# Cross-attention planner: rank by reader backlog, new places for the side work, values wait for their context

## The chip, the cores and the metric

The kernel runs on one core of a Trainium2 chip. The time is device time in microseconds (us), the median over several executions; less is better. The engines of the core are TensorE (PE; its weight loads are PEld), VectorE (DVE), ScalarE (ACT), GpSimd (POOL), and SyncE (SP), which here issues all DMAs. [...]

## What is computed

Two decoder layers over 16 batch elements. `x` is (16, 256, 128), the context `ctx_1024` is (16, 1601, 128), all float32. There are 16 heads of 8.

```python
# layer 0
x = layernorm(x + attn(x, x, x, causal))
x = layernorm(x + attn(x, ctx, ctx))                 # 256 queries, 1601 keys
x = layernorm(x + moe(x))                            # 8 experts of 512, top 2, exact gelu
# layer 1
h = x + mha(rmsnorm(x), rmsnorm(x), rmsnorm(x), self_mask)
h = h + mha(rmsnorm(h), ctx, ctx, cross_mask)
out = h + moe_ffn(rmsnorm(h))                        # 8 silu experts, top 2, and one shared expert
```

Every softmax is an exact one with its row maximum taken off; the experts are computed densely and weighted (`comb`), with zero weight for those not picked.

## The kernel before, in words

The work is cut into rounds, t = -1 to 32. Round t does the cross-attention of one batch element (layer 0 for t = 0 to 15, layer 1 for t = 16 to 31) and beside it side work for its neighbours: the experts of the element of round t-1, and for the element of round t+1 the self-attention, the keys, the values, the moves of the keys and, in layer 1, the masks; loads of `x` and of the context for round t+2.

The cross-attention is the backbone. For each of four head groups g (four heads) and each of seven pairs of key tiles i there is a beat of four score tiles `SC` [g.i] (line 939; in layer 1 a mask is put in first by line 929), whose readers are exponentials on ACT (`probs_c`, line 1226), and one or two steps `WV` that add the sums of the pair before (line 957). The row maxima that these scores need come one round earlier, from chunks `MC` (line 828): scores once more, in the other orientation, read by DVE as maxima (line 1069 in layer 0, line 1075 in layer 1, where the mask is added). There are 96 chunks of 512 keys and 16 tails of 68 keys in a round. A matmul of `SC` or `MC` uses 32 of the 128 rows of the array, so four heads run at the same time.

Other step names: `XT` transposes `x` (846) for ACT to copy; `QP` makes queries and keys of the self-attention and the queries of the cross-attention from it (852), which DVE adds a bias to and POOL splits in two; `KC` and `VC` make keys and values from the context (986, 990); `KD` moves the keys of one head group by twelve DMAs (1335); `MS`, `SS`, `WS` are maxima, scores and sums of the self-attention (873 to 913); `OT`, `OPT`, `OPM` transpose and project an attention's result; `EF` and `ES` are the two halves of an expert (1016, 1028), whose weights are loaded by `EL` (1347) into two slots each; `CL` loads the context (1325).

Seven PSUM banks are shared by all steps but the sums. A step waits until the reader of its bank's last user (DVE for some kinds, ACT for others) is done. All engines run their instructions in the program's order.

The order is set while the program is built, by a planner. `weave` holds one queue of steps for each kind of side work and one for the backbone, spreads each queue over the round by the table `WHEN` (begin and end as shares of the round, times `LENGTH`), and takes step after step: among the heads of the queues that are within `AHEAD` us of the earliest due one, the one with the least `idle + NEAR * place`, where `idle` comes from `Model`, a cost model of TensorE, its readers and the banks. To each beat it adds up to `MOST` chunks `MC` while banks are free in the model within `SOON` us; and `behind`, with `SLACK` chunks of tolerance, adds a beat of chunks alone after a score beat when the maxima are late.

The lines of the planner that matter:

```python
            trial = Model(model)
            idle = sum(trial.add(x) for x in piece)
            if best is None or idle + NEAR * place < best[0]:
                best = idle + NEAR * place, which
```

Of the kernel before, what the change touches and what calls it, by code (L numbers as in the profile page):

```python
# [65 lines left out]
def spans(n, step):  # L66
    return [(a, min(step, n - a)) for a in range(0, n, step)]
# [83 lines left out]
BY_READER = {"OPM": ("x_in", "mid", "stored"), "EBM": ("xe",), "ES": ("xe", "comb"), "MC": ("mask",)}  # L151


LENGTH = (145.1, 143.0)


class Model:
# [128 lines left out]

NEAR, AHEAD, SOON, MOST, SLACK = 0.0485, 53.3, 0.42, 4, 4


def weave(plan, length, *lists):
# [4 lines left out]
    for begin, end, steps in lists:  # L297
        timed = spaced(steps)
        total, done, queue = sum(cost for _, cost in timed), 0.0, []
        for x, cost in timed:  # L300
            place = length * (begin + (end - begin) * (done + cost_of(x) / 2) / total)
# [28 lines left out]
    while any(queues):  # L330
        follow()
        soonest = min(queue[-1][0] for queue in queues if queue)
        best = None
        for which, queue in enumerate(queues):
            if not queue or queue[-1][0] > soonest + AHEAD:
                continue
            place, piece = queue[-1]
            own = {id(x) for x in piece}
            if any(id(y) in pending - own for x in piece for y in x.of.values()):
                continue  # L340
            trial = Model(model)
            idle = sum(trial.add(x) for x in piece)
            if best is None or idle + NEAR * place < best[0]:
                best = idle + NEAR * place, which
        if best is None:
            steps = [plan.follow.pop(0)] if plan.follow else beat_of(plan.pull(model, pending, MOST, True))
            put(steps)
            continue
        _, piece = queues[best[1]].pop()
        put(piece)  # L350
        scores = [x for x in piece if x.kind == "SC"]
        if scores and plan.behind(scores[-1]):
            follow()
            steps = plan.pull(model, pending, MOST)
            if steps:
                put(beat_of(steps))
# [3 lines left out]
def beat_of(steps):  # L360

    for n, x in enumerate(steps):
        x.beat, x.led = steps, n > 0
    return steps
# [309 lines left out]
def numbered(order):  # L674
# [4 lines left out]
    for x in order:  # L679
# [22 lines left out]
    return order  # L702


WHEN = [{"experts": (0.3, 1.0), "keys": (0.049, 0.375), "values": (0.21, 0.706), "self": (0.01, 0.692), "load": (0.398, 0.739), "context": (0.914, 0.924)},
        {"experts": (0.114, 0.97), "keys": (0.124, 0.276), "values": (0, 0.439), "self": (0.029, 0.786), "load": (0.507, 0.886), "context": (0.775, 0.876), "cross masks": (0.283, 0.787), "self masks": (0.764, 0.88)}]


def round_of(plan, t):

    side = []
    if t >= 1:
        begin, end = WHEN[(t - 1) // B]["experts"]
        side += [(begin, end, plan.experts((t - 1) // B, (t - 1) % 2)),
                 (end, end + 0.01, plan.store((t - 1) % 2, (t - 1) % B))]
    if t + 1 < LAST:
        l, p, b = (t + 1) // B, (t + 1) % 2, (t + 1) % B
        when = WHEN[l]
        if t < 0:
# [18 lines left out]
    if t < 0:  # L738
        return weave(plan, LENGTH[0], *side) + plan.first_maxima()
    if t == LAST:  # L740
        sums = plan.last_sums()
        for x in sums:
            plan.model.add(x)
        return sums + weave(plan, LENGTH[1], *side)
    return weave(plan, LENGTH[t // B], (0, 1, attended), *side)


# [20 lines left out]
def nth(x):  # L768

    return x.n + 1  # L770
# [62 lines left out]
def tensor_program(pe, T, M, order):  # L833
    for x in order:
# [148 lines left out]
        elif x.kind == "KC":  # L983
            if "ctx" in x.of:
                pe.wait_ge(M["ctx_loaded"], 16 * nth(x.of["ctx"]))
            pe.matmul(tile[:, 0:x.kn], T["w_key"][:, x.l, :], T["ctxT"][:, x.k0:x.k0 + x.kn], start=True,
                      stop=True).then_inc(M["d_made"], 1)
        elif x.kind == "VC":
            for n, (k0, kn) in enumerate(spans(SK, P)[x.i:x.i + 3]):
                last = pe.matmul(tile[0:kn, n * VCOLS:(n + 1) * VCOLS], T["ctxT"][:, k0:k0 + kn], T["w_val"][:, x.l, 1, :],  # L990
                                 start=True, stop=True)
# [18 lines left out]
        elif x.kind == "EF":  # L1010
            load = x.of["load"]
# [7 lines left out]
        elif x.kind == "ES":  # L1019
            load, hid = x.of["load"], T["hidden"][x.i % 2]  # L1020
# [589 lines left out]
```

## Time and profile before

| | us |
|---|---|
| median of 3 executions | 4880.08 |
| lowest, highest | 4859.92, 4895.96 |
| the profiled execution, whole | 4873.83 |
| its span in the trace | 4872.4 |

| engine | busy us | share of the span |
|---|---|---|
| PE | 4629.5 | 95% |
| PEld | 2838.4 | 58% |
| DVE | 3616.2 | 74% |
| ACT | 2697.6 | 55% |
| POOL | 698.4 | 14% |

A busy PE is not PE at its peak, since matmuls overlap and their ends are modelled. [...] Where a wait is put down to an engine that had long been done, a DMA is what ended it.

### The profile page before, as it was taken

The page shows a single profiled execution, that of the slowest core. Times are in us where ns is not written, and L with a number is a line of the kernel's source. Part 1 is how long each engine was busy: PE and PEld are TensorE (multiplying, and loading weights), DVE is VectorE, ACT ScalarE, POOL GpSimd, SP SyncE. Part 2 cuts the span into 40 slices and gives each one's busy share as a digit, 9 for nine tenths or more (in the row PEclk, how much of TensorE's full clock was granted, in tenths as well). Part 3 has the DMA queues.
Part 4 walks back from the last instruction along what each step waited for, and adds up shares of the span by engine and source line. Part 5 has one row for each costly group of instructions (what it writes and reads, how often), then busy time and mean ns, then how long its engine had stood idle before and what let it go on. Part 6 is the DMA issues. An engine that isn't in the chain of part 4 may idle for free.

```text
span 4872.4 us, 105117 instructions
## 1 busy us (share of the span) xinstructions
PE 4629.5 (95%) x41312; PEld 2838.4 (58%) x41312; DVE 3616.2 (74%) x9823; ACT 2697.6 (55%) x5505; POOL 698.4 (14%) x853
## 2 busy tenths in 40 slices
PE   6999999999999999999999999999999999999999
PEld 3465556665556666555555556555565556655566
DVE  5766776667776767777667887778777887778875
ACT  1566556666666666665564544545455544555454
POOL 2111111211111221111111011011110111010100
PEclk8899999999999999999999999999999999999999
DMA  2122222222222222223333333323333223332322
GB/s 66 38 52 53 44 52 62 63 51 51 52 51 61 60 65 51 51 46 81 77 77 77 81 79 81 80 75 80 79 89 79 74 71 91 89 77 70 76 61 72
DMA packets 168007, 327.20 MB, mean 67 GB/s; under 512 B 25656, under 2 KB 76624, under 8 KB 167520
## 3 DMA queue, kind: packets, MB, share of 16 engines
q1 hardware_dynamic: 167520, 320.49, 26.9%
q8 instruction: 332, 5.44, 0.5%
q14 instruction: 155, 1.27, 0.1%
HBM read 237.40 MB, written 4.19 MB: 50 GB/s over the span
## 4 chain that ended last, share of the span: by engine, by line
PE 76%; DVE 18%; ACT 3%; issue 1%; POOL 0%; DMA 0%; DVEq 0%
PE sums L957 15%; PE b L1028 11%; PE b L1016 10%; PE b L828 9%; PE b L929 8%; PE b L939 7%; DVE chunk_max L1069 6%; PE b L852 4%; DVE b L1075 4%; DVE nm_s L1058 4%; PE b L913 2%; ACT probs_c L1226 2%; PE b L880 2%; PE b L904 1%; PE b L873 1%; PE b L885 1%
## 5 line engine op out<-in xcount | busy, mean ns | idle before, releaser
L1226 ACT ACTIVATE probs_c<-b 128x512 f32<-128x512 f32 (+1 forms) x3584 | 1737.5, 570 | 1368.1 <-PE b L939 1363.3
L1075 DVE CUSTOM_DVE_ANT_0 b<-b,mcross_q 128x512 f32<-128x512 f32 (+1 forms) x2048 | 1120.3, 606 | 234.8 <-PE b L828 230.9
L1069 DVE TENSOR_REDUCE chunk_max<-b 128x1 f32<-128x512 f32 x1536 | 969.1, 683 | 136.0 <-PE b L828 134.7
L957 PE MATMUL sums<-probs_c,vc 128*32 128x256 f32 x13312 | 932.7, 395 | 0.3 <-ACT probs_c L1226 0.3
L828 PE MATMUL b<-kc,qc 32*128 32x512 f32 (+1 forms) x4096 | 805.9, 411 | 15.3 <-DVE tmp_s L1087 2.0
L1028 PE MATMUL b<-w_back,hidden 128*128 128x128 f32 x4352 | 567.0, 283 | 25.5 <-DVE chunk_max L1069 20.2
L1028 PEld LDWEIGHTS b<-w_back,hidden 128*128 128x128 f32 x4352 | 536.5, 196 | 84.2 <-ACT probs_c L1226 31.4
L939 PE MATMUL b<-qc,kc 32*128 32x256 f32 (+1 forms) x6656 | 544.4, 339 | 29.2 <-DVE chunk_max L1069 11.4
L957 PEld LDWEIGHTS sums<-probs_c,vc 128*32 128x32 f32 x13312 | 347.2, 111 | 342.3 <-issue 160.5
L828 PEld LDWEIGHTS b<-kc,qc 32*128 32x128 f32 x4096 | 419.9, 187 | 213.1 <-ACT probs_c L1226 61.6
L1208 DVE SCALAR_TENSOR_TENSOR xe<-b,comb,xe 128x128 f32<-128x128 f32 x544 | 186.1, 349 | 478.0 <-PE b L1028 477.8
L1016 PE MATMUL b<-xT_e,w_in 128*128 128x256 f32 x2176 | 529.6, 388 | 7.0 <-ACT probs_s L1221 6.7
L939 PEld LDWEIGHTS b<-qc,kc 32*128 32x128 f32 (+1 forms) x6656 | 321.6, 183 | 339.0 <-issue 188.0
L929 PE MATMUL b<-mcross_k,ident_b 128*128 128x512 bf16 (+1 forms) x1792 | 469.2, 369 | 30.4 <-DVE k_lo L1126 8.0
L1016 PEld LDWEIGHTS b<-xT_e,w_in 128*128 128x128 f32 x2176 | 398.0, 191 | 95.6 <-ACT probs_c L1226 22.8
L1221 ACT ACTIVATE probs_s<-b 128x512 f32<-128x512 f32 x512 | 278.4, 597 | 257.8 <-PE b L891 257.2
L1058 DVE TENSOR_REDUCE nm_s<-b 128x2 f32<-128x512 f32 x512 | 329.0, 685 | 85.7 <-PE b L885 84.2
L929 PEld LDWEIGHTS b<-mcross_k,ident_b 128*128 128x128 bf16 (+1 forms) x1792 | 172.4, 100 | 231.0 <-DVE chunk_max L1075 60.2
L1075 DVE DVE_READ_ACCUMULATOR2_ANT chunk_max<- 128x1 f32 x2048 | 290.5, 142 | 0.0
L1249 ACT ACTIVATE hidden<-b 128x512 f32<-128x512 f32 x288 | 171.9, 597 | 165.4 <-PE b L1016 164.8
L1301 POOL TENSOR_TENSOR rstd_s<-mean_var_s,halves 128x2 f32<-128x2 f32 x32 | 31.6, 988 | 1590.7 <-DVE mean_var_s L1116 1590.7
L1245 ACT ACTIVATE hidden<-b,b_hid 128x256 f32<-128x256 f32 x512 | 206.4, 477 | 89.4 <-PE b L1016 87.3
(159 smaller groups left out, 4564.9 us busy)
## 6 DMA issues: line engine op xcount, KB each, us to landing
w_in<-in_experts SPq DMA_DIRECT2D x272, 256.0 KB, 3.3
w_back<-in_experts SPq DMA_DIRECT2D x272, 256.0 KB, 3.0
kc<-k_hi SPq DMA_DIRECT2D x1024, 50.0 KB
ctxT<-in_ctxT SPq DMA_DIRECT2D x32, 800.5 KB, 6.2
kc<-k_lo SPq DMA_DIRECT2D x512, 50.0 KB
mask_words<-in_mcross SPq DMA_DIRECT2D x32, 800.5 KB
mask_words<-in_mcrossT SPq DMA_DIRECT2D x32, 768.0 KB
out_x<-xe SPq DMA_DIRECT2D x32, 128.0 KB, 1.8
```

Of the source, the lines that this page charges most:

```text
L828: last = pe.matmul(tile[:, n * y.kn:(n + 1) * y.kn], T["qc"][y.p][rows, y.g, qt * P:(qt + 1) * P], T["kc"][rows, y.g, y.k0:y.k0 + y.kn], s ...
L929: pe.matmul(tile_of(T, y)[0:y.kn, 0:n * S], T["ident_b"][0:y.kn, 0:y.kn], mask, start=True, stop=False)
L939: last = pe.matmul(tile_of(T, y)[0:y.kn, half * S:(half + 1) * S], T["kc"][rows, y.g, kt * P:kt * P + y.kn], T["qc"][y.p][rows, y.g, :], s ...
L957: last = pe.matmul(acc[HP * j:HP * j + HP, :], T["vc"][x.p][0:x.kn, v0:v0 + HP], probs_of(T, x)[0:x.kn, j, half:half + S], start=x.j == 0, ...
L1016: last = pe.matmul(tile[:, half * S:(half + 1) * S], T["w_in"][load.slot][:, f * P:(f + 1) * P], T["xT_e"][:], start=True, stop=True)
L1028: last = pe.matmul(tile[:, 0:D], hid[:, f, x.c * P:(x.c + 1) * P], T["w_back"][load.slot][:, f * D:(f + 1) * D], start=f == 0, stop=f == N ...
L1058: dve.tensor_reduce(maxima[:, x.j, :, MROW], tile.rearrange("p (q k) -> p q k", q=QT), AX, ALU.max, negate=True).then_inc(M["d_read"], 1)
L1069: done = dve.tensor_reduce(best[:, x.i:x.i + 1], tile, AX, ALU.max)
L1075: done = dve.tensor_tensor_reduce(part, part, mask, 1.0, -3e38, ALU.add, ALU.max, best[:, qt:qt + 1])
L1221: act.activation(T["probs_s"][:, x.j, :], tile, ACT.Exp, scale=SCALE).then_inc(M["a_read"], 1)
L1226: act.activation(probs_of(T, x)[0:x.kn, x.j, 0:n], tile[0:x.kn, 0:n], ACT.Exp, scale=SCALE).then_inc(M["a_read"], 1)
L1245: done = act.activation(T["hidden"][x.i % 2][:, f, :], tile[:, half * S:(half + 1) * S], ACT.Gelu, bias=T["b_hid"][:, x.i, f:f + 1])
```

## The change

The planner's rank gains a term: after a trial it looks how far the clocks of DVE and ACT in the model are ahead of TensorE's by more than 1 us, and adds `HEAVY` times that. `DRY` would do the same for readers that are behind, and is 0. The constants and both tables are new (for layer 1 the context load moves from shares 0.775 to 0.876 of the round to 0.49 to 0.668), and `VC` now waits until its context has landed, where it is told which load that is; the number and shape of the matmuls, reads and DMAs are the same, and only their order differs.

```diff
-LENGTH = (145.1, 143.0)
+LENGTH = (140.4, 145.8)
...
-NEAR, AHEAD, SOON, MOST, SLACK = 0.0485, 53.3, 0.42, 4, 4
+NEAR, AHEAD, SOON, MOST, SLACK = 0.0436, 167.5, 0.32, 3, 2
+HEAVY, DRY = 0.091, 0
...
-            if best is None or idle + NEAR * place < best[0]:
-                best = idle + NEAR * place, which
+            rank = idle + NEAR * place
+            for busy in (trial.dve, trial.act):
+                rank += HEAVY * max(0, busy - trial.pe - 1.0) + DRY * max(0, trial.pe - busy)
+            if best is None or rank < best[0]:
+                best = rank, which
...
-WHEN = [{"experts": (0.3, 1.0), "keys": (0.049, 0.375), "values": (0.21, 0.706), "self": (0.01, 0.692), "load": (0.398, 0.739), "context": (0.914, 0.924)},
+WHEN = [{"experts": (0.207, 1.0), "keys": (0.177, 0.426), "values": (0.198, 0.975), "self": (0.08, 0.58), "load": (0.358, 1.0), "context": (0.95, 1.0)},
...
         elif x.kind == "VC":
+            if "ctx" in x.of:
+                pe.wait_ge(M["ctx_loaded"], 16 * nth(x.of["ctx"]))
```

The changed kernel's line numbers are 4 higher at the chunks, the scores and the sums (832, 943, 961), and 6 higher at values and experts (996, 1022, 1034). In the rows below `b` is a PSUM bank, `kc` and `qc` are the keys and queries of the cross-attention, and the number behind x counts matmuls.

**Place 1: TensorE in a steady round of layer 0, from the expert 6 to the second half of expert 7.** Before:

```order
L1028 MATMUL b<-w_back,hidden 128x128 x8
L939 MATMUL b<-qc,kc 128x256 x8
L828 MATMUL b<-kc,qc 128x512 x3
L957 MATMUL sums<-probs_c,vc 32x256 x4
L1028 MATMUL b<-w_back,hidden 128x128 x8
L939 MATMUL b<-qc,kc 128x256 x8
```

After:

```order
L1034 MATMUL b<-w_back,hidden 128x128 x8
L943 MATMUL b<-qc,kc 128x256 x8
L832 MATMUL b<-kc,qc 128x512 x3
L961 MATMUL sums<-probs_c,vc 32x256 x4
L996 MATMUL b<-w_val,ctxT 65x144
L1034 MATMUL b<-w_back,hidden 128x128 x4
L943 MATMUL b<-qc,kc 128x256 x8
L832 MATMUL b<-kc,qc 128x512 x3
L961 MATMUL sums<-probs_c,vc 32x256 x8
L1034 MATMUL b<-w_back,hidden 128x128 x4
```

Between the first half of expert 7 (`w_back`, x4 is one `ES` step) and the sums before it now stands the last, small piece of the values (`w_val`, 65x144), and the two `ES` steps of expert 7, which stood together, are a score beat apart. A few rows ahead, a beat of three chunks stands where the transposes of the maxima (`nm_c`) stood. The loads on SP stand in the same order in both programs: the twelve moves of head group 2, the `w_back` of expert 7, the context.

**Place 2: TensorE from the last maxima of a layer-0 round into the next round.** Before:

```order
L939 MATMUL b<-qc,kc 65x256 x4
L828 MATMUL b<-kc,qc 128x512 x2
L957 MATMUL sums<-probs_c,vc 32x256 x8
L904 MATMUL b<-ident,nm_c 128x128 x2
L828 MATMUL b<-kc,qc 128x512 x4
L846 MATMUL b<-ident,x_in 128x128 x2
L852 MATMUL b<-xT_s,w_pad 128x256 x2
L939 MATMUL b<-qc,kc 128x256 x8
L828 MATMUL b<-kc,qc 128x512
L957 MATMUL sums<-probs_c,vc 32x256 x4
L852 MATMUL b<-xT_s,w_pad 128x256 x6
L939 MATMUL b<-qc,kc 128x256 x8
```

After:

```order
L961 MATMUL sums<-probs_c,vc 32x256 x8
L908 MATMUL b<-ident,nm_c 128x128 x2
L832 MATMUL b<-kc,qc 128x512 x3
L850 MATMUL b<-ident,x_in 128x128 x2
L943 MATMUL b<-qc,kc 128x256 x8
L832 MATMUL b<-kc,qc 128x512
L961 MATMUL sums<-probs_c,vc 32x256 x4
L856 MATMUL b<-xT_s,w_pad 128x256 x2
L943 MATMUL b<-qc,kc 128x256 x8
L832 MATMUL b<-kc,qc 128x512 x2
L961 MATMUL sums<-probs_c,vc 32x256 x8
L856 MATMUL b<-xT_s,w_pad 128x256 x4
```

Before, the first projection (`w_pad`) stood right behind the transpose of `x_in`, and three more a beat later. Now a score beat and a sum stand between the transpose and the first projection, and the four come one, two and one, with score beats between.

**Place 3: TensorE in a steady round of layer 1, behind score beat [0.4].** Before:

```order
L828 MATMUL b<-kc,qc 128x512 x4
L975 MATMUL b<-ident,tmp_e 128x128 x2
L986 MATMUL b<-ctxT,w_key 128x401
L990 MATMUL b<-w_val,ctxT 128x144 x3
L980 MATMUL b<-w_out,oT_e 128x128 x2
L873 MATMUL b<-mself_q,ident_b 128x512 x2
L885 MATMUL b<-ks,qs 128x256 x4
L828 MATMUL b<-kc,qc 128x68 x4
L986 MATMUL b<-ctxT,w_key 128x398
L873 MATMUL b<-mself_q,ident_b 128x512 x2
L885 MATMUL b<-ks,qs 128x256 x4
L828 MATMUL b<-kc,qc 128x68 x4
```

After:

```order
L832 MATMUL b<-kc,qc 128x512 x2
L832 MATMUL b<-kc,qc 128x68 x2
L996 MATMUL b<-w_val,ctxT 128x144 x3
L984 MATMUL b<-w_out,oT_e 128x128 x2
L877 MATMUL b<-mself_q,ident_b 128x512 x2
L889 MATMUL b<-ks,qs 128x256 x4
L832 MATMUL b<-kc,qc 128x68 x6
L877 MATMUL b<-mself_q,ident_b 128x512 x2
L889 MATMUL b<-ks,qs 128x256 x4
L832 MATMUL b<-kc,qc 128x512
```

Before, two beats of self-attention maxima, two pieces of keys and two of values stood with eight tails and four chunks in a stretch without a score beat. Now one piece of values stands there, and the keys follow two score beats later, among the self-attention's scores. Over a round, beats that hold maxima chunks alone are 7 before and 11 after, in either layer.

## Rows read from the trace of the kernel before

**Rows 1.** The page: span, PE's total, PE's clock in 40 slices, the ending chain by engine.

```profile
span 4872.4 us, 105117 instructions
PE 4629.5 (95%) x41312; PEld 2838.4 (58%) x41312; DVE 3616.2 (74%) x9823; ACT 2697.6 (55%) x5505; POOL 698.4 (14%) x853
...
PEclk8899999999999999999999999999999999999999
...
PE 76%; DVE 18%; ACT 3%; issue 1%; POOL 0%; DMA 0%; DVEq 0%
```

**Rows 2.** The chain in order of time, a mark once a round: start, length, what.

```profile
384.05 3.58 DVE chunk_max L1069 x6
...
530.68 3.59 DVE chunk_max L1069 x6
...
1117.63 3.58 DVE chunk_max L1069 x6
...
1258.17 3.59 DVE chunk_max L1069 x6
```

**Rows 3.** Stretches, one round each: PE, PEld, DVE, ACT, POOL busy, clock, DMA share, GB/s.

```profile
660.70:807.20 146.50, 139.22 (x1231) 87.11 (x1227) 102.10 (x224) 90.45 (x184) 24.47 (x29) 0.94 0.24 54
...
1245.40:1384.90 139.50, 133.55 (x1230) 84.09 (x1226) 101.87 (x225) 90.46 (x184) 24.46 (x29) 0.99 0.25 57
...
3631.40:3785.20 153.80, 149.49 (x1361) 90.52 (x1357) 123.32 (x389) 77.95 (x160) 18.82 (x24) 1.00 0.31 80
```

**Rows 4.** Stretches, 3.4 us each, around the end of a layer-0 round.

```profile
800.35:803.76 3.41, 3.31 (x36) 1.93 (x32) 2.98 (x9) 3.07 (x8) 0.00 (x0) 0.91 0.00 0
803.76:807.18 3.42, 3.42 (x24) 1.18 (x22) 1.79 (x5) 0.19 (x1) 0.00 (x0) 0.50 0.41 45
...
814.00:817.42 3.42, 3.42 (x10) 2.50 (x8) 1.38 (x2) 0.00 (x0) 1.84 (x2) 0.59 0.81 292
817.42:820.83 3.41, 3.41 (x42) 2.04 (x41) 2.69 (x5) 2.57 (x6) 3.24 (x5) 1.00 0.01 2
```

**Rows 5.** Timeline of SP, 770 to 783 us: the moves of a head group, then loads.

```profile
773.66 0.65 SPq L1335 DMA_DIRECT2D kc<-k_hi  x1
...
782.16 0.44 SPq L1347 DMA_DIRECT2D w_back<-in_experts  x1
782.70 0.56 SPq L1325 DMA_DIRECT2D ctxT<-in_ctxT  x1
```

**Rows 6.** Timeline of PE, 781 to 800 us.

```profile
783.62 0.64 PE L957 MATMUL sums<-probs_c,vc 65*32 65x256 f32 x8
785.78 3.50 PE L1028 MATMUL b<-w_back,hidden 128*128 128x128 f32 x16 [1.52 <-DVE chunk_max L1069]
```

**Rows 7.** Issues 781 to 789 us: size, time to landing.

```profile
w_back<-in_experts SPq DMA_DIRECT2D x1, 256.0 KB, 3.5
```

**Rows 8.** Issues 3720 to 3722 us: a load behind a group's moves, no load after it.

```profile
w_in<-in_experts SPq DMA_DIRECT2D x1, 256.0 KB, 4.1
```

**Rows 9.** Issues 769.5 to 771 us: a load with no moves ahead of it.

```profile
w_back<-in_experts SPq DMA_DIRECT2D x1, 256.0 KB, 2.6
```

**Rows 10.** Timeline of PE, 806.5 to 818 us: the first projections of a round.

```profile
808.44 2.05 PE L852 MATMUL b<-xT_s,w_pad 128*128 128x256 f32 x4 [0.56 <-ACT xT_s L1219]
```

**Rows 11.** Timeline of PE: a beat of chunks alone, layer 0, and what follows.

```profile
1374.96 0.50 PE L828 MATMUL b<-kc,qc 32*128 32x512 f32 x4
1375.31 0.62 PE L939 MATMUL b<-qc,kc 32*128 32x256 f32 x3
```

**Rows 12.** The same in layer 1.

```profile
3770.29 0.51 PE L828 MATMUL b<-kc,qc 32*128 32x512 f32 x4
3770.73 1.56 PE L1016 MATMUL b<-xT_e,w_in 128*128 128x256 f32 x6
```

**Rows 13.** Stretches: the part of a round with the self-attention, layer 1 and layer 0.

```profile
3652.40:3688.90 36.50, 33.42 (x301) 17.06 (x299) 32.26 (x109) 16.81 (x37) 2.15 (x4) 1.00 0.18 41
...
1256.80:1315.10 58.30, 54.21 (x521) 28.73 (x520) 50.30 (x113) 31.65 (x68) 3.82 (x6) 1.00 0.09 13
```

**Rows 14.** Issues 3755 to 3762 us: the context load of layer 1.

```profile
ctxT<-in_ctxT SPq DMA_DIRECT2D x1, 800.5 KB, 6.9
```

More of the change, by code:

```diff
@@ L702, in numbered @@
     return order
-WHEN = [{"experts": (0.3, 1.0), "keys": (0.049, 0.375), "values": (0.21, 0.706), "self": (0.01, 0.692), "load": (0.398, 0.739), "context": (0.914, 0.924)},
-        {"experts": (0.114, 0.97), "keys": (0.124, 0.276), "values": (0, 0.439), "self": (0.029, 0.786), "load": (0.507, 0.886), "context": (0.775, 0.876), "cross masks": (0.283, 0.787), "self masks": (0.764, 0.88)}]
+WHEN = [{"experts": (0.207, 1.0), "keys": (0.177, 0.426), "values": (0.198, 0.975), "self": (0.08, 0.58), "load": (0.358, 1.0), "context": (0.95, 1.0)},
+        {"experts": (0.079, 1.0), "keys": (0.293, 0.368), "values": (0.119, 0.401), "self": (0.029, 0.629), "load": (0.5, 0.656), "context": (0.49, 0.668), "cross masks": (0.393, 0.779), "self masks": (0.786, 0.796)}]
 def round_of(plan, t):
```

## Prediction

> **What bounds the kernel now.** I read the page first. PE is busy in 95% of the span, and the chain that ended last runs over PE for 76% and over DVE for 18% [rows 1]. So PE is the bound, and DVE takes turns with it. The change adds and removes no matmul of the real work, so it can only win in three places: PE's idle time, time in which PE runs at half clock, and the small costs of turning from one kind of matmul to another.
>
> The marks of the chain give the length of a round in layer 0: 146.6 us from 384.05 to 530.68, the same mean over the next four (586.95 / 4 = 146.7), then 140.5 [rows 2]. The stretches by round say why. A round of 146.5 us had a granted clock of 0.94 and one of 139.5 us had 0.99, with the same busy time on DVE, ACT and POOL [rows 3]. A clock of 0.94 means 12% of 146.5, 17.6 us, at half speed, which loses 8.8; 0.99 means 2.8 us, which loses 1.4; 7.4 us between them, against 7.0 seen. So at full clock a layer-0 round is about 138 us, and the clock takes 0 to 9 us more. In layer 1 a round is 153.8 us at a clock of 1.00, with PE not busy for 4.3 us [rows 3]; no clock loss is to be had there.
>
> Where does the clock fall? In the last 3.4 us of a round PE was busy for 3.31, but with maxima, tails and sums; then it ran at 0.50, and it was back at full only after a stretch of nothing but projections (814.00, PE 3.42 in 10 records) [rows 4]. One more short fall follows the wait before expert 7.
>
> **The change part by part.** All terms are for steady rounds: 15 of layer 0 and 14 of layer 1. What the first two and the last two rounds do I take as unchanged.
>
> 1. *The wait before expert 7, layer 0 (place 1).* PE waits 1.52 us before that `ES` step [rows 6]. The page's row names DVE, but the load of `w_back` was issued at 782.16 and took 3.5 us, so it landed at 785.7, and PE began at 785.78 [rows 5, 7]. It was issued late because twelve moves, from 773.66 on, stood ahead of it on SP [rows 5]. That order is the same after. What changes is PE's side: a beat of chunks alone in place of the transposes, and the small values step, which is half a us at most. I take 0.4 us less wait: 15 x 0.4 = -6 us. The lower bound is nothing, the upper 15 x 1.5 = -23.
> The context load stood 0.54 us behind the `w_back` [rows 5] and now waits for the last values step. A lone load landed in 2.6 us [rows 9], so one could hope for another 0.9 us a round. But a load behind moves and with nothing after it took 4.1 [rows 8]: the moves ahead cost it, not the context behind, and I count nothing for this. [...]
>
> 2. *The transpose at the start of a layer-0 round (place 2).* The projection waited 0.56 us for ACT's copy of the transpose [rows 10]. After, a score beat and a sum stand between them and cover it: 15 x -0.56 = -8 us. The bound on the other side: the score beat now comes first and may wait for banks instead, 0.
>
> 3. *More beats of chunks alone.* 11 a round instead of 7. One costs PE 0.35 us in layer 0 (1374.96 to 1375.31) and 0.44 in layer 1 (3770.29 to 3770.73) [rows 11, 12]. Where DVE is behind they are free, since PE would have waited anyway. In layer 0 four of the 11 stand in the self-attention's part, where before had none: one more is exposed. In layer 1 three of 11 stand there, and one did before: I take two exposed. So 15 x 0.35 + 14 x 0.88 = +5 + 12 = +17 us. Ends: none exposed, 0; all four, 15 x 1.4 + 14 x 1.76 = +46.
>
> 4. *Layer 1, where DVE falls behind (place 3).* The part with the self-attention took 36.5 us, with PE busy for 33.42 and DVE for 32.26 [rows 13]: 3.1 us in which PE had nothing it could start, out of 4.3 in the round. Before, maxima, keys and values stood in one lump for DVE; after, keys stand two score beats later and chunks come at most three at a time. This is what the new term in the rank is for. I take two thirds of the 3.1 us, as DVE's work is not less and the stretch remains its densest: 14 x -2.0 = -28. Ends: 0 and 14 x -3.1 = -43.
>
> 5. *The same part in layer 0.* 58.3 us with PE busy for 54.21 and DVE for 50.30 [rows 13]. The same work stays in it but one or two values pieces, so DVE has about 0.6 us less to do: 15 x -0.6 = -9. Ends: 0 and 15 x -4.1 = -61.
>
> 6. *The wait of the values.* In layer 0 a keys step, which waits for the same load, stands ahead, and it costs nothing. In layer 1 the context load took 6.9 us from its issue [rows 14]; it moves earlier by a third of a round and the first values step moves later, so it has tens of us of cover. 0. Its earlier place puts it among expert loads, which have a beat or more of slack; 0.
>
> 7. *The clock in layer 0.* The weak spot, the end of the round, has the same light steps as before; what follows is spread thinner (place 2) but the wait before expert 7 is a bit less. I can't say which way this goes, so 0, with 7 us a round either way.
>
> Sum: -6 - 8 + 17 - 28 - 9 = -34 us. The profiled execution took 4873.8 us (its span and 1.4 us around it), so 4840 us. The median of before, 4880.1, is 6 above the profiled one, which is inside its own spread of 36.
>
> **The rivals.**
>
> *A: slower by a longer stretch at half clock (chance 0.15).* After the fall the clock came back only when projections filled a stretch [rows 4]. After the change the projections come one, two, one, with light beats between. If recovery therefore waits for the dense part some 14 us further on, each such round loses 7 us more: 15 x 7 = +105, so 4840 + 105 = 4945. It decides from 34 / 15 = 2.3 us a round on, that is 4.5 us more at half clock in every round. For it: place 2, and the round of 146.6 repeating itself five times over [rows 2]. Against it: a clock that stays up until then owes nothing, and sums fill the gaps.
>
> *B: faster by clock (0.22).* If the falls at the round's end go away as they did in the 139.5 us round [rows 3], the six rounds of 146.7 and a few like them win 7 us each: 7 x 7 = -49, so 4840 - 49 = 4791. For it: the rounds of 139.5 and 140.5 us ran the very same order [rows 2, 3], so it hangs on little. [...]
>
> *C: nothing to gain (0.23).* DVE's work in the dense parts is the same, terms 4 and 5 come to nothing, and all four beats are exposed: -6 - 8 + 46 = +32, so 4906, or with two exposed 4877. I take 4880 for it.
>
> **How the numbers follow.** My forecast has 0.40, and its own range is 4815 to 4865. A 0.15, B 0.22, C 0.23. The range for 8 in 10 is 4775 to 4905: it takes in B and C and leaves most of A out. About 1% (49 us) is what a measurement of this kernel can tell from no change: faster than 4831 is B and a third of the forecast, with some of the deeper ends of terms 4 and 5: 0.38; slower than 4929 is most of A: 0.13; between them 0.49.
>
> **What would show it.** Term 1: the wait before the first `ES` step of expert 7 is 1.0 to 1.2 us. Term 2: no wait at the round's first projection. Terms 3 and 4: a layer-1 round of 152 to 153 us at a clock of 1.00, with PE not busy for about 2.5 us. Terms 5 and 7: marks of the chain 136 to 145 us apart in layer 0. A shows as a clock of 0.90 or less by round; B as 0.98 or more in nearly all. I am wrong if layer-1 rounds are longer than 154 us, or if new waits of DVE for mask words appear there, where their loads now stand close behind a group's moves.

## The result, and the profile after

| | before | after |
|---|---|---|
| median, us | 4878.5 of 4 | 4742.3 of 4 |
| lowest, highest | 4859.9, 4896.0 | 4731.1, 4752.6 |
| the profiled execution's span | 4872.4 | 4745.7 |

The ratio is 0.972, with an interval of 0.968 to 0.976: 2.8% less. The forecast was 4840 us with a range from 4775 to 4905, so the time lies outside it, on the fast side.

The page after the change, its span, PE's total and the ending chain by engine; they answer to [rows 1]. 366 matmul records are missing of 41312 in this trace, so PE's idle time in it is a little too large.

```profile
span 4745.7 us, 104925 instructions
PE 4555.6 (96%) x40946; PEld 2804.6 (59%) x41312; DVE 3607.6 (76%) x9823; ACT 2699.7 (57%) x5505; POOL 696.7 (15%) x853
...
PE 79%; DVE 14%; ACT 3%; issue 2%; SPq 0%; DMA 0%; POOL 0%; DVEq 0%
```

The granted clock is the share of its full speed that TensorE was given. In the trace before, cut from 800 to 822 us into stretches of 0.4 us, it was 1.00 in 20 of them and 0.50 in 33, and in the two at a change 0.91 and 0.52. "Half clock" is the 0.50, and the figure of a longer stretch is read as a mean of the two. At 0.50 four matmuls of the projection took 2.05 us (808.44, [rows 10]), at 1.00 they take 1.13 (1200.46, below).

DVE and ACT did the same work in the same time. DVE's share of the chain went from 18% to 14%. Stretches of one round each, three of layer 0 and one of layer 1 (busy time of PE, PEld, DVE, ACT, POOL, granted clock, DMA share, GB/s), beside [rows 3]:

```profile
358.70:496.40 137.70, 130.79 (x1221) 82.34 (x1218) 101.98 (x225) 90.90 (x186) 24.38 (x29) 1.00 0.26 59
775.00:919.50 144.50, 140.06 (x1222) 86.10 (x1227) 102.11 (x225) 90.81 (x186) 24.42 (x29) 0.93 0.24 55
1196.20:1332.40 136.20, 131.37 (x1222) 82.79 (x1226) 101.72 (x224) 90.74 (x186) 24.42 (x29) 1.00 0.26 58
...
3072.20:3223.20 151.00, 147.80 (x1341) 90.09 (x1356) 122.93 (x389) 77.91 (x161) 18.82 (x24) 1.00 0.32 81
```

A layer-0 round at a clock of 1.00 now takes 136.2 to 137.7 us, and 12 of the 15 take 136 to 142; one of those left is the 144.5 us at a clock of 0.93, and the last takes 151.8. The layer-1 rounds take 149.8 to 151.3 us, nearly all of them 151.0. I cut both traces at the same instruction, once a round, and took half of the time at half clock as the loss by clock. The 126.7 us of the two spans then go as follows:

| part | before | after | of it by clock | the rest |
|---|---|---|---|---|
| rounds -1 and 0 | 217.9 | 214.1 | -2.7 | -1.1 |
| layer 0, rounds 1 to 15 | 2173.4 | 2103.2 | -30.2 | -40.0 |
| round 16, where layer 1 begins | 158.5 | 151.7 | -2.9 | -3.9 |
| layer 1, rounds 17 to 30 | 2159.6 | 2113.8 | -10.2 | -35.6 |
| the end | 162.9 | 162.9 | -1.7 | +1.7 |

So 48 us of the gain are clock by this reckoning, and 79 are time in which PE waited. Half of the half-clock time is taken as an upper figure: two pairs of runs below, with and without one wait, give 0.3 in place of 0.5, a third pair 0.5. So the clock's part is 30 to 48 us, and the waits' part 79 to 97.

Which waits went? In layer 1, rounds 17 to 30, PE waited for these readers (total us, times, longest); `b` is a bank, a tile of 128x512 float32 that matmuls write and DVE or ACT reads. Before, and behind it after:

```profile
PE b L873 <- ACT probs_s L1221: 10.3, 27, 0.5
PE b L986 <- DVE k_lo L1126: 9.7, 13, 0.8
PE b L929 <- DVE k_lo L1126: 8.0, 12, 0.7
...
PE b L933 <- ACT probs_s L1227: 10.2, 28, 0.5
PE b L933 <- DVE chunk_max L1081: 3.5, 14, 0.3
```

The 18 us for DVE's reads of the keys (`k_lo`) are gone. With all lines together, PE's waits for ACT's exponentials of the self-attention (`probs_s`) fell from 23 to 10.5 us in these rounds, and from 26 to 12 in layer 0. So a third of the waits that went were for ACT, which no term of the prediction names in the dense parts.

The places of the prediction, in the trace after. The load of expert 7: the timeline of SP and then of PE, and behind it the issue with its time to landing. They answer to [rows 5 to 7].

```profile
1168.80 0.66 SPq L1341 DMA_DIRECT2D kc<-k_hi  x1
...
1177.20 0.44 SPq L1353 DMA_DIRECT2D w_back<-in_experts  x1
1180.00 0.33 SPq L1331 DMA_DIRECT2D ctxT<-in_ctxT  x1
...
1179.51 0.46 PE L996 MATMUL b<-w_val,ctxT 128*65 128x144 f32 x2
1180.77 1.65 PE L1034 MATMUL b<-w_back,hidden 128*128 128x128 f32 x8 [0.80 <-DVE chunk_max L1075]
```

```profile
w_back<-in_experts SPq DMA_DIRECT2D x1, 256.0 KB, 3.5
```

The load still stands behind the twelve moves and still takes 3.5 us; 1177.20 + 3.5 = 1180.7, when PE goes on. The context load now stands 2.8 us behind it in place of 0.54, and the 3.5 us are the same: what is behind a load doesn't hold it up here, as term 1 took. The wait is 0.80 us here and 1.17 us as a mean over rounds 2 to 14; rounds 1 and 15 have none. The start of a round, PE (beside [rows 10]), has no wait for the transpose:

```profile
1198.00 0.50 PE L832 MATMUL b<-kc,qc 32*128 32x512 f32 x3
1198.43 0.44 PE L850 MATMUL b<-ident,x_in 128*128 128x128 f32 x2
1198.90 0.93 PE L943 MATMUL b<-qc,kc 32*128 32x256 f32 x8
1199.57 0.40 PE L832 MATMUL b<-kc,qc 32*128 32x512 f32 x1
1199.89 0.64 PE L961 MATMUL sums<-probs_c,vc 65*32 65x256 f32 x8
1200.46 1.13 PE L856 MATMUL b<-xT_s,w_pad 128*128 128x256 f32 x4
```

But the score beat behind it takes 0.93 us, where an unhindered one takes 0.51 (1201.52 in the same trace): its second half begins 0.43 us late. From the transpose to the end of that beat it is 1.41 us, in every round that is at full clock there. So of the 0.56 us only some 0.14 are won.

And the parts with the self-attention, layer 1 (24.0 us into the round, as in [rows 13]) and layer 0 (13.2 us into it):

```profile
3096.20:3132.70 36.50, 35.04 (x308) 18.19 (x308) 32.45 (x103) 15.94 (x34) 2.14 (x4) 1.00 0.01 2
...
1209.40:1267.70 58.30, 55.48 (x518) 28.50 (x523) 50.73 (x118) 32.10 (x69) 5.70 (x7) 1.00 0.09 15
```

DVE is as busy in them as before, and PE waits for 1.5 us in place of 3.1, and for 2.8 in place of 4.1.

### The profile page after: what moved, and what is told of

It is laid out like the page before. It is cut to its first block, busy times and chain, and to the rows that moved or that the text cites. A ratio compares the mean times of both kernels' runs of the same rounds, so it can differ in the third digit from the quotient of the medians.

```text
span 4745.7 us, 104925 instructions
## 1 busy us (share of the span) xinstructions
PE 4555.6 (96%) x40946; PEld 2804.6 (59%) x41312; DVE 3607.6 (76%) x9823; ACT 2699.7 (57%) x5505; POOL 696.7 (15%) x853
## 4 chain that ended last, share of the span: by engine, by line
PE 79%; DVE 14%; ACT 3%; issue 2%; SPq 0%; DMA 0%; POOL 0%; DVEq 0%
PE sums L961 16%; PE b L1022 10%; PE b L1034 10%; PE b L832 9%; PE b L943 7%; PE b L933 7%; DVE chunk_max L1075 5%; PE b L856 4%; PE b L917 3%; DVE nm_s L1064 3%; DVE b L1081 3%; PE b L884 2%; ACT probs_c L1232 2%; PE b L996 2%; PE b L908 2%
## 5 line engine op out<-in xcount | busy, mean ns | idle before, releaser
L832 PE MATMUL b<-kc,qc 32*128 32x512 f32 (+1 forms) x4096 | 822.1, 412 | 17.4 <-DVE chunk_max L1075 7.1
L1034 PE MATMUL b<-w_back,hidden 128*128 128x128 f32 x4352 | 565.4, 281 | 15.5 <-DVE vc L1138 12.0
L943 PE MATMUL b<-qc,kc 32*128 32x256 f32 (+1 forms) x6656 | 515.0, 336 | 17.3 <-DVE chunk_max L1077 2.2
L943 PEld LDWEIGHTS b<-qc,kc 32*128 32x128 f32 (+1 forms) x6656 | 302.7, 182 | 300.6 <-issue 185.5
L933 PE MATMUL b<-mcross_k,ident_b 128*128 128x512 bf16 (+1 forms) x1569 | 403.2, 364 | 32.8 <-ACT probs_s L1227 10.9
L1207 DVE SCALAR_TENSOR_TENSOR hidden<-hidden,b 128x512 f32<-128x512 f32 x288 | 193.6, 686 | 101.8 <-ACT hidden L1255 101.8
```

The lines of the kernel that those rows point to most:

```text
L832: last = pe.matmul(tile[:, n * y.kn:(n + 1) * y.kn], T["qc"][y.p][rows, y.g, qt * P:(qt + 1) * P], T["kc"][rows, y.g, y.k0:y.k0 + y.kn], s ...
L933: pe.matmul(tile_of(T, y)[0:y.kn, 0:n * S], T["ident_b"][0:y.kn, 0:y.kn], mask, start=True, stop=False)
L943: last = pe.matmul(tile_of(T, y)[0:y.kn, half * S:(half + 1) * S], T["kc"][rows, y.g, kt * P:kt * P + y.kn], T["qc"][y.p][rows, y.g, :], s ...
L1034: last = pe.matmul(tile[:, 0:D], hid[:, f, x.c * P:(x.c + 1) * P], T["w_back"][load.slot][:, f * D:(f + 1) * D], start=f == 0, stop=f == N ...
```

## The experiments

Every run is set against runs of the kernel before on the same chip; there that kernel's median was 4888 to 4892 us. The changed kernel's own 4742 was taken beside 4878, so against the others it stands for some 10 us more; the ratios hold that already. "Full clock" is the mean length of a round less half of its time at half clock; a difference of some 0.3 us means nothing. Each row's round lengths are of one traced execution, and where half costs too much (above), the last figure flatters a row with much time at half clock. b_heavy and b_heavy_w compute something else than the reference; what, is told under the values' wait.

| kernel | median | ratio, interval | layer 0: round, at half clock, full clock | layer 1: round, full clock |
|---|---|---|---|---|
| before | 4888 to 4892 | 1 | 144.9, 12.9, 138.4 | 154.3, 153.5 |
| b_chunks3 | 4883 | 0.998, 0.997 to 1.000 | 143.5, 10.7, 138.2 | 157.3, 155.1 |
| b_heavy | 4916 | 1.004, 1.002 to 1.006 | 146.5, 18.1, 137.4 | 155.6, 154.9 |
| b_heavy_w | 4914 | 1.005, 1.002 to 1.007 | 145.1, 15.0, 137.6 | 155.5, 154.9 |
| b_tables | 4898 | 1.002, 1.000 to 1.003 | 145.6, 17.0, 137.1 | 154.9, 154.0 |
| p_const_heavy | 4873 | 0.997, 0.995 to 0.998 | 141.9, 11.1, 136.3 | 156.7, 153.2 |
| p_tables_heavy | 4903 | 1.002, 1.001 to 1.004 | 144.6, 14.6, 137.3 | 154.9, 154.9 |
| a_flat | 4869 | 0.995, 0.993 to 0.996 | 145.4, 16.3, 137.2 | 153.8, 153.8 |
| s_flat | 4931 | 1.009, 1.006 to 1.012 | 148.8, 22.7, 137.4 | 153.2, 153.2 |
| a_chunks4 | 4857 | 0.994, 0.992 to 0.996 | 144.3, 15.4, 136.6 | 152.5, 152.5 |
| after | 4742 | 0.972, 0.968 to 0.976 | 140.2, 8.9, 135.8 | 151.0, 151.0 |
| h_008 | 4754 | 0.973, 0.970 to 0.975 | 140.5, 8.4, 136.3 | 151.1, 151.1 |
| h_01 | 4737 | 0.969, 0.966 to 0.972 | 138.8, 6.2, 135.6 | 151.4, 151.4 |
| a_h1 | 4771 | 0.977, 0.974 to 0.980 | 139.7, 7.7, 135.8 | 153.3, 153.3 |
| a_h2 | 4779 | 0.978, 0.975 to 0.980 | 140.0, 8.6, 135.7 | 153.4, 153.0 |
| b_start | 4881 | 0.999, 0.997 to 1.001 | 145.5, 14.0, 138.5 | 154.2, 153.4 |
| b_load | 4837 | 0.989, 0.987 to 0.992 | 142.5, 11.4, 136.8 | 154.2, 153.3 |
| a_load | 4712 | 0.964, 0.961 to 0.966 | 138.2, 5.7, 135.3 | 151.0, 151.0 |
| l_most4 | 4862 | 0.995, 0.992 to 0.997 | 143.2, 13.2, 136.6 | 153.7, 153.1 |
| h01_load | 4706 | 0.963, 0.961 to 0.965 | 137.0, 3.6, 135.2 | 151.4, 151.4 |

**One part of the change at a time.** Theory S held that the limit of three chunks carries the gain, R that the rank does, T that the tables do.

```diff
-NEAR, AHEAD, SOON, MOST, SLACK = 0.0485, 53.3, 0.42, 4, 4
+NEAR, AHEAD, SOON, MOST, SLACK = 0.0485, 53.3, 0.42, 3, 2
```

> The kernel before with one line of constants changed: at most three chunks to a beat and a tolerance of two (MOST, SLACK = 3, 2 in place of 4, 4). Theory S (short beats): the gain of layer 1 comes from this alone, since a fourth chunk asks for a bank that VectorE has not read yet; then layer-1 rounds take 151 to 152 us in place of 153.8, layer-0 rounds lose one or two us of waiting, and the time is 4810 to 4830. Theory R (rank) and theory T (tables): the limit of three only adds beats of chunks alone, 4880 to 4900, layer-1 rounds at 154 us or more.

> The kernel before with the new term in the rank alone (HEAVY 0.091), tables and constants as before. Theory R (rank): most of the gain is here, 4790 to 4820, layer-1 rounds at 151 to 152 us. Theory S (short beats) and theory T (tables): within 10 us of 4880.

> The kernel before with the new LENGTH and WHEN and the wait of the values for their context, constants and rank as before. Theory T (tables): most of the gain is here, 4780 to 4810, layer-0 rounds at 138 us with hardly a stretch at half clock. Theory S (short beats): only the layer-0 part, 4850 to 4870, layer-1 rounds still 153 to 154 us. Theory R (rank): 4880.

```diff
-HEAVY, DRY = 0.091, 0
+HEAVY, DRY = 0, 0
```

> The changed kernel with the new term of the rank at zero (HEAVY 0), all else as changed. Theory R (rank): it falls back to 4820 to 4850. Theory S (short beats) and theory T (tables): it stays within 20 us of the changed kernel, 4740 to 4765, layer-1 rounds at 151 to 152 us.

All three theories fell. No part gives even half a per cent by itself, and the rank alone costs 0.4%. Yet without the rank (a_flat) the ratio is 0.995 in place of 0.972: four fifths of the gain are gone.

**Pairs, and neighbours.**

> The kernel before with the new constants and the new rank, and the wait of the values; the tables WHEN and LENGTH stay as before. Theory P (a pair carries it, this one): rank and limit of three work together whatever the tables say, 4750 to 4790, layer-1 rounds at 151 to 152 us. Theory Z (the order as a whole): no part and no pair has a value of its own, 4830 to 4910, layer-1 rounds at 153 us or more.

> The changed kernel with the constants NEAR, AHEAD, SOON, MOST, SLACK of before; tables and rank as changed. Theory P (a pair carries it, this one): 4750 to 4790. Theory Z (the order as a whole): 4820 to 4900. The rank alone gave 4916 against 4890, so if rank and tables need each other, this is the run that shows it.

> The changed kernel with HEAVY 0.08 in place of 0.091. The order of layer 1 stays all but the same, that of layer 0 is another one (a fifth of its steps stand elsewhere). Theory M (the rank term works as a rule): layer 0 stays at 139 us a round, 4735 to 4760. Theory Z (the order as a whole): layer-1 rounds at 151 us, layer-0 rounds back at 142 to 145 us, 4780 to 4830.

> The changed kernel with HEAVY 0.10 in place of 0.091. The order of layer 0 stays the same, a tenth of layer 1's steps stand elsewhere. Theory M (the rank term works as a rule): layer 1 stays at 151 us a round, 4735 to 4760. Theory Z (the order as a whole): layer-1 rounds at 153 to 154 us, 4770 to 4800.

The pairs fell to theory Z: within some 15 us of before. The neighbours went the other way, to theory M: with another weight of the rank the ratio is 0.973 and 0.969, although a fifth of layer 0's steps, or a tenth of layer 1's, stand elsewhere. So the gain is not one lucky order, as far as one other order for each layer can show it. It belongs to all three parts together. Neighbours of the tables were not tried, and `NEAR`, `AHEAD` and `SOON` never by themselves: with `MOST` and `SLACK` of before the changed kernel has 0.994 (a_chunks4, below), with all five constants of before 1.002, so those three carry another 0.8%.

**Why one part alone gives nothing, at one place.** The next run makes only the change of place 2 in the kernel before (braces hold a beat, and `RS` is a short step of POOL).

```diff
-XT RS QP {SC[0.0] MC} WV QP QP QP
+XT RS {SC[0.0] MC} WV QP QP QP QP
```

> The kernel before with one thing moved in layer 0: the round's first projection stands behind the first score beat and its sums, as in the changed kernel. By term 2 of the prediction 14 x 0.56 = 8 us less: 4880 beside 4888. Theory G (this start is what holds the clock): the falls of 13.7 us at the round's end become short or vanish, 4830 to 4860. Rival A of the prediction: the half-clock stretch grows, 4900 to 4950.

It can't be told from no change. PE at the start of a round of b_start:

```profile
1236.92 0.50 PE L839 MATMUL b<-kc,qc 32*128 32x512 f32 x4
1237.35 0.44 PE L857 MATMUL b<-ident,x_in 128*128 128x128 f32 x2
1238.20 0.38 PE L950 MATMUL b<-qc,kc 32*128 32x256 f32 x2 [0.41 <-DVE chunk_max L1080]
1238.80 0.50 PE L950 MATMUL b<-qc,kc 32*128 32x256 f32 x6 [0.22 <-DVE chunk_max L1080]
```

The wait for the transpose, 0.56 us, is gone, and the score beat waits 0.41 and 0.22 us for banks instead, whose reader is DVE. This is so in the eight of 14 rounds that begin at full clock; in the six at half clock the marked wait is 0.16 us. From the transpose to the end of the beat it is 1.95 us at full clock, against 1.41 in the changed kernel.

Four chunks stand ahead of it here and three in the changed kernel (1198.00 above), so one could think that the limit of three makes the difference. It doesn't. l_most4, with four chunks at the same place:

```profile
1211.63 0.50 PE L843 MATMUL b<-kc,qc 32*128 32x512 f32 x4
1212.06 0.44 PE L861 MATMUL b<-ident,x_in 128*128 128x128 f32 x2
1212.43 1.04 PE L954 MATMUL b<-qc,kc 32*128 32x256 f32 x8
```

The same 1.41 us, in 11 of its 14 rounds, and a_chunks4 has them too at full clock. So the wait moves from one place to the next, and what takes it away in the changed orders lies elsewhere; this stays open. Over layer 0 PE's idle time in b_start is 112.3 us, against 114.4.

**The limit of three.**

> The changed kernel with MOST, SLACK = 4, 4 in place of 3, 2, and all else as changed: beats of chunks alone fall from 11 to 9 in layer 0 and to 7 in layer 1. By term 3 of the prediction, which priced four more of them at 17 us, it would be 4725. Theory S (short beats help, since a fourth chunk asks for a bank that VectorE has not read yet): layer-1 rounds of 152.5 us or more, 4765 to 4810.

> The kernel that gave 4712 us (the changed one with the expert 7 load ahead of the moves) with MOST 4 in place of 3 and nothing else: beats of chunks alone fall from 11 to 9 and to 7. By term 3 of the prediction 15 to 17 us less, 4695. Theory S (a beat of three is better than fewer beats of four): 4730 to 4830, with layer-1 rounds of 152 us or more.

With four chunks allowed the beats of chunks alone fall from 11 to 9 in layer 0 and to 7 in layer 1, and the time rises by some 105 us against the changed kernel and by 150 against a_load. Four more such beats, which I priced at 17 us, come with a gain in this company. PE's busy time speaks against the price too: 149.5 us in a layer-1 round with 11 of them (a_load, below, whose trace has every record) and 149.5 with 7 [rows 3].

Not all of it are waits. Of the 101 us between the traces of a_chunks4 and the changed kernel 62 are in layer 0, which has 98 us more at half clock: seven of its rounds end with a fall of 20.5 us. Between l_most4 and a_load 76 of 128 us are in layer 0, with 113 us more at half clock. In layer 1, rounds 17 to 30, the traces differ by 20.5 us at a clock of 1.00, and there the waits for banks that DVE reads are seen. The largest two of a_chunks4:

```profile
PE b L933 <- DVE chunk_max L1081: 14.6, 28, 0.8
PE b L933 <- DVE nm_s L1064: 11.2, 16, 0.7
```

The first is 3.5 us in the changed kernel (above), the second 0.2. So in layer 1 the fourth chunk costs waits for DVE's banks, as theory S held; in layer 0 about half of the loss or more goes with the clock.

**The lump in layer 1.** Without the rank term the planner puts three values pieces and all four keys pieces between score beats [0.3] and [0.4]. PE in a_flat there, some of the keys and the values, and what waits behind them:

```profile
3036.14 1.00 PE L996 MATMUL b<-w_val,ctxT 128*128 128x144 f32 x6 [0.16 <-DVE chunk_max L1081]
3036.98 0.84 PE L990 MATMUL b<-ctxT,w_key 128*128 128x401 f32 x2
3037.65 0.90 PE L996 MATMUL b<-w_val,ctxT 128*128 128x144 f32 x6
3038.39 0.84 PE L990 MATMUL b<-ctxT,w_key 128*128 128x401 f32 x2
...
3041.55 0.90 PE L933 MATMUL b<-mcross_k,ident_b 128*128 128x512 bf16 x3 [0.28 <-DVE k_lo L1132]
3043.27 0.39 PE L933 MATMUL b<-mcross_k,ident_b 128*128 128x512 bf16 x1 [0.82 <-DVE k_lo L1132]
```

The kernel before has the same pattern:

```profile
3040.46 0.94 PE L986 MATMUL b<-ctxT,w_key 128*128 128x398 f32 x2 [0.75 <-DVE k_lo L1126]
...
3044.85 0.39 PE L929 MATMUL b<-mcross_k,ident_b 128*128 128x512 bf16 x1 [0.71 <-DVE k_lo L1126]
```

A plain rule spreads the pieces without the rank term:

```diff
+            rank += 3.0 * crowd * (piece[0].kind in ("KC", "VC"))
...
+        crowd = 0 if piece[0].kind == "SC" else crowd + (piece[0].kind in ("KC", "VC"))
```

> The changed kernel with HEAVY 0 and, in its place, a plain rule: a keys or values piece is ranked 3 us worse for every such piece placed since the last score beat. Without the rank term seven of these pieces stood in one lump of layer 1 between score beats [0.3] and [0.4]; with the rule they stand one at a time. Theory L (the lump): spreading keys and values is what the rank term does for layer 1, so its rounds fall from 154.0 to 151 to 152 us, and the time to 4800 to 4840. Theory Q (the rank does more): layer-1 rounds stay at 153 us or more, 4855 to 4880.

Theory L fell: the waits at that place went (PE's idle time from 4.2 to 2.8 us a round), but the round is only 0.6 us shorter, since PE was busy for 0.8 us more; why, I can't say. In all s_flat is slower than a_flat, 1.009 against 0.995, because the rule holds in layer 0 too, where the time at half clock rises from 245 to 340 us. Then the rank term in one half of a layer-1 round alone:

> The changed kernel, but in layer 1 the rank term is on only for the first 14 of a round's 28 score beats (the part with the self-attention, the keys and the values); from beat [2.0] on the order is that of the kernel with HEAVY 0. Layer 0 is untouched. With the term a layer-1 round takes 151.0 us, without it 154.0. Theory L (the first half, where the lump was): 151.3 to 152 us, 4745 to 4755 in all. Theory E (the second half, the experts): 153 us or more, 4770 to 4785.

> The counterpart: in layer 1 the term is on only from score beat [2.0] on, and the first half is that of HEAVY 0, lump included. Theory L: 153 to 154 us a round, 4770 to 4785. Theory E: 151.3 to 152 us, 4745 to 4755. If neither half carries it alone, both runs are at 152.5 us, 4765.

Each half gives 0.4 to 0.8 us and both 2.8. The traces name a wait that belongs to the second half, some 134 us into the round, for DVE's sum of an expert (`xe`). It is there in a_flat, in s_flat and in a_h1, in this order, and neither in a_h2 nor in the changed kernel:

```profile
PE b L933 <- DVE xe L1214: 10.1, 13, 1.8
...
PE b L936 <- DVE xe L1217: 11.2, 13, 1.9
...
PE b L934 <- DVE xe L1215: 12.2, 10, 2.2
```

The waits for the keys' readers (`k_lo`, 18.3 us in a_flat) are gone in a_h1. In a_h2, which still has the lump, they are 1.4 us, so the lump doesn't make them alone; PE waits for `probs_s` there instead, 21.4 us in the three largest rows. In a_h1 the keys and values are spread as in the changed kernel, but the round takes over its chunks from another second half, and the last ones of the first head group come one beat later: the exponentials of beat [1.0] begin 37.2 us behind the round's first in place of 35.7. So the halves hang together by the chunks; that this is all of it isn't shown. And all this is layer 1, 39 of the 123 us between the traces of a_flat and the changed kernel. The larger piece, 78 us, is in layer 0, with 112 us less at half clock, and no run takes apart what the rank does there.

**The load of expert 7.** The term that the prediction counted at 6 us, with 23 as its end, tried by itself: the twelve moves go behind the load.

```diff
-KD(g2) EF6 EF6 ES5 ES5 EL7
+EF6 EF6 ES5 ES5 EL7 KD(g2)
```

> The kernel before with one thing moved in layer 0: the load of expert 7's w_back stands ahead of the twelve moves of head group 2 in place of behind them. By term 1 of the prediction its wait of 1.5 us goes: 15 x 1.5 = 23 us, 4865. Theory K (the wait also costs clock): the short fall of 3.4 us behind it goes too, 12 x 1.7 = 20 us more, and perhaps some of the long ones at the round's end: 4800 to 4845. Rival: the moves are late instead, or the wait was VectorE's all along: 4885 to 4895.

> The changed kernel with the same thing moved. Its wait before expert 7 is 1.17 us, so 15 x 1.2 = 18 us less: 4725. Theory K (the wait also costs clock): the short falls 122 to 127 us into a round go as well, 4705 to 4720. Rival: nothing, 4742.

b_load: the timeline of SP, then of PE, and behind it the issue with its time to landing:

```profile
762.38 0.33 SPq L1358 DMA_DIRECT2D w_back<-in_experts  x1
762.80 0.65 SPq L1346 DMA_DIRECT2D kc<-k_hi  x1
...
766.73 0.64 PE L968 MATMUL sums<-probs_c,vc 65*32 65x256 f32 x8
767.32 2.05 PE L1039 MATMUL b<-w_back,hidden 128*128 128x128 f32 x16
```

```profile
w_back<-in_experts SPq DMA_DIRECT2D x1, 256.0 KB, 2.6
```

It lands 2.6 us after its issue and PE doesn't wait. The 16 matmuls take 2.05 us, where they took 3.50 [rows 6] at a clock of 0.54, after 1.00 from 784 to 786 us: the clock fell behind the wait, so the wait cost twice. This holds for most rounds: in the kernel before 14 rounds have the wait and 11 of them a fall at it (three with 1.8 us of wait have none), and in b_load no round has either there. b_load is 53 us faster than before by the medians and 38 by the traces; the traced execution of before lies 16 us under its median on this chip. In its trace layer 0 is 36 us shorter, 24.8 of them at full clock, where the bound of the term was 23 and the 15 waits sum to 25.2, and 11 by clock. The load took 3.5 us behind the moves [rows 7] and takes 2.6 ahead of them; how the moves held it up isn't shown. On the changed kernel the same edit gives 30 us by the medians, some 40 by the ratios. Its waits there sum to 15.2 us, and all are gone. Layer 0 is 30.7 us shorter in the trace, with 47.8 us less at half clock; half of that and the waits would be 39. So the clock gave 15.5 us here, 0.3 for each us at half clock. (h_01 and h01_load say the same: 26.1 us, waits of 15.4, and 39.1 us less at half clock.) Two rounds of a_load, one of each layer:

```profile
1042.00:1178.50 136.50, 133.45 (x1227) 83.12 (x1226) 101.73 (x225) 90.77 (x186) 24.51 (x29) 0.99 0.26 58
...
3040.40:3191.50 151.10, 149.51 (x1359) 89.97 (x1356) 122.78 (x389) 78.01 (x161) 18.89 (x24) 1.00 0.32 81
```

> The changed kernel with HEAVY 0.10 and, in layer 0, the load of expert 7's w_back ahead of the twelve moves. Layer 0 then has the order of the run that gave 4712 us, layer 1 one that measured 151.7 us a round in place of 151.0. If the gains add: 4712 + 14 x 0.7 = 4720, less what chance in the clock gives; 4700 to 4725.

4706 us lies in that range. But by the ratio, 0.963 beside 0.964, it can't be told from a_load: the two share the place of the best version here, 3.7% faster than before.

**The values' wait.** In the order of b_heavy one thing is computed otherwise.

> The kernel before with the new term in the rank, as in the run that gave 4916 us, and now with the wait of the values for their context as well: in that order nothing else holds the first values step of a layer-1 round back until its context has landed, and what that run computed had old context in it. By term 6 of the prediction the wait costs nothing: 4905 to 4925. Rival: the values were early by so much that the wait costs a part of the context load's 7.2 us in 15 rounds, 4940 to 5010.

The wait costs nothing there. But what I wrote of old context was wrong, since the wait changes nothing in what is computed. The plan shows the cause: at the start of layer 1 the transposes of the last layer-0 element's result (OT) stand behind the first head group's last sums of the next element, and ACT has written into the same buffer (o_c) by then. The trace of b_heavy bears it out: in round 16 ACT writes it at 44.4 us and the transposes read it from 48.9 on; in the kernel before they read it at 30.0, and ACT writes at 42.0. Every instruction is still there, so the times stand. With the old tables the rank term alone thus gives an order that can't be used.

## Why the prediction was wrong, point by point

The forecast had 34 us less waiting and nothing by clock; the traces have 79 to 97 and 30 to 48. Either alone would have stayed in the range: 79 to 97 us of waits give 4777 to 4795, and the forecast's 34 with 48 by clock 4792. So two steps failed, the sum of the waits (terms 3 and 5 above all) and the 0 for the clock (term 7), and the range took the second for a rival of the first.

- *Term 1, the wait before expert 7* (-6): the wait went from 1.61 to 1.17 us as a mean over rounds 2 to 14, 0.44 where 0.4 was taken, and in rounds 1 and 15 it is gone: 25.2 to 15.2 us in all. Right, and a little short. What I didn't count is the half clock behind the wait: a fall follows 11 of the 14 waits in the kernel before, and none is there in b_load.
- *Term 2, the first projection* (-8): the wait is gone, but the score beat that covers it ends 0.42 us later than an unhindered one, so it is some 2 us and not 8. In b_start the beat is later still, and the edit alone is worth nothing, the term's other bound. The term named this bound and took the full 0.56.
- *Term 3, beats of chunks alone* (+17): a step that failed. The price isn't there: PE is busy for 149.5 us in a layer-1 round with 7 such beats and with 11. And I left out what comes with them: I priced a turn of PE and not the bank that a fourth chunk asks for. Allowing it again costs 105 to 150 us, in layer 1 by waits for DVE's banks, in layer 0 to about half or more by the clock.
- *Term 4, the dense part of layer 1* (-28): PE's idle time in that stretch fell from 3.1 to 1.5 us, and to 1.05 in a_load, where no record is missing: -2.0 us a round, as taken. Over the whole round at full clock it is 153.5 to 151.0 us, 2.5 less; terms 3 and 4 together had 1.1.
- *Term 5, the same in layer 0* (-9): mis-sized. Idle time 4.1 to 2.8 us, and 2.3 in a_load, 1.3 to 1.8 a round where 0.6 was taken. I let DVE's load stand for PE's waits; the load is the same (50.3 and 50.7 us), only its spacing changed, and much of what went is the wait for ACT's `probs_s` (26 to 12 us over layer 0).
- *Term 6, the values' wait* (0): right.
- *Term 7, the clock* (0): the other step that failed. By half of the half-clock time -30 us in layer 0, and -10 in layer 1, where I had written that nothing was to be had. This is rival B at 0.22, which gave 49 us, though by its own mark, 0.98 or more in nearly all rounds, it came only in part: four of the 15 rounds have that, as before, and the long falls at the round's end went from eight to one. The range treated the forecast and B as ways that exclude each other, though fewer waits and fewer falls came together.
- *The sum* (-34): -127 in the traces, -48 by clock and -79 by waits, if half of the half-clock time is counted. The waits are 22 us short in layer 0 (18 forecast, 40 measured), of which 5 are term 3, 10 to 18 term 5 and 4 term 1, less 6 for term 2, and 20 short in layer 1 (16 and 36), of which 12 are term 3 and 7 what lies outside the stretch of term 4 (14 x 0.5).
- Rival A didn't come: no round has a clock under 0.93 after round 0 but the last of layer 0. The marks that I asked for were seen: rounds of 136 to 145 us in layer 0 but for the last, and 151.0 in layer 1, which is less than the 152 to 153 forecast.

## What to carry to other kernels

When TensorE waits in many small places for the same readers, an edit that removes one wait can be worth nothing, since the wait may come back one step on (in b_start 0.56 us went and 0.63 us came, at a ratio of 0.999); or it can be worth 1.5 to 2 times its length (in b_load the waits were 25.2 us, and the gain 38 us by the traces and 53 by the medians). Look at what stands behind it. Judge a planner's rules together, and try the neighbours of a setting before calling it luck. A load that is late behind a row of moves is worth moving by itself, even for 1.5 us, if the clock falls behind the wait, as it did here in 11 of 14 rounds. And count a wait at its place with the half-clock time behind it, not beside it.

## What the runs showed of the hardware

At the end of a layer-0 round the clock used to fall with PE busy for 3.31 of 3.41 us [rows 4]. In the changed kernel it held through stretches with less. Stretches of 3.4 us there:

```profile
1190.40:1193.80 3.40, 3.20 (x39) 1.87 (x39) 3.17 (x6) 2.88 (x6) 3.13 (x5) 1.00 0.01 2
1193.80:1197.20 3.40, 3.22 (x43) 1.89 (x47) 2.78 (x9) 2.84 (x8) 0.00 (x1) 1.00 0.12 39
1197.20:1200.60 3.40, 3.31 (x37) 1.42 (x29) 3.40 (x8) 1.22 (x3) 0.73 (x1) 1.00 0.48 62
```

And in a_load it fell behind a stretch that was as busy as the first two:

```profile
1073.70:1077.10 3.40, 3.23 (x19) 1.44 (x18) 3.40 (x7) 2.42 (x8) 0.00 (x0) 1.00 0.02 5
1077.10:1080.50 3.40, 3.40 (x31) 1.33 (x34) 2.66 (x9) 0.39 (x2) 1.50 (x2) 0.54 0.00 0
```

So PE's busy time in one such stretch doesn't tell whether the clock falls. Falls at that place that lasted 13.7 us or more were seen in eight of 15 rounds before, and in one after. In b_load, where the wait before expert 7 is gone, there are eight as well, so that wait is not their cause. What is, stays open. The clock is also a large piece of chance here: after and h_01 run the same order in their steady layer-0 rounds, and their traces have 133 and 94 us at half clock in layer 0.

Matmuls that use 32 of the array's rows overlapped: one such chunk took 0.39 us (3768.97 in the trace before) and a beat of four 0.51 [rows 12]. And SP issued its DMAs in the program's order: the moves of a head group from 773.66 us on and `w_back` behind them at 782.16 [rows 5], and in b_load `w_back` at 762.38 and the moves from 762.80 on.
